# FFN down projection of a decoder layer: a wait for each inner piece, and the sum of squares inside a tile's product

## The reference

```
x = x + ffn(layernorm(x))
gate, up = split(x_ln @ ternary(w_gate_up).T)      # 2 x 2048
h   = silu(gate) * up                              # 896 rows x 2048
hn  = h * rsqrt(mean(h*h) + eps)
out = hn @ ternary(w_proj).T                       # 2048 -> 512
```

## Time and profile before

| | |
|---|---|
| median of 3 runs | 1248.84 us (1247.83 to 1251.47) |
| the profiled execution | 1249.16 us |
| its span, first to last instruction | 1247.4 us |
| mean granted clock of TensorE | 0.978 |
| FFN products, first L1150 to last L1218 | 1071 to 1245 us |

### The profile page before, as it was taken

One profiled execution on the slowest core, in us unless ns is written; L12 is line 12 of the kernel. 1 busy time (PEld: TensorE's weight loads), 2 busy tenths in 40 slices (PEclk: granted clock), 3 DMA queues, 4 the chain that ended last, 5 costly groups with the idle time before them and its releaser, 6 DMA issues.

```text
span 1247.4 us, 19243 instructions
## 1 busy us (share of the span) xinstructions
PE 1177.8 (94%) x6330; PEld 782.0 (63%) x6330; DVE 934.7 (75%) x2785; ACT 804.9 (65%) x2295; POOL 619.6 (50%) x769
## 2 busy tenths in 40 slices
PE   4999989889999999999999999999999998898998
PEld 2667766556666666666666676666667666454563
DVE  4669988999889888798999976557777877464241
ACT  4666557777778886667666775567777677662230
POOL 2537875644544555555556732126444445266171
PEclk9989989899999999999999999999999999999999
DMA  8210001212110221213233121041011110000000
GB/s 266 86 58 26 24 17 33 84 35 69 52 51 18 64 93 47 76 43 105 89 109 94 60 87 38 17 144 59 27 50 60 42 35 1 1 1 0 35 1 26
DMA packets 27475, 69.26 MB, mean 56 GB/s; under 512 B 2944, under 2 KB 9216, under 8 KB 27376
## 3 DMA queue, kind: packets, MB, share of 16 engines
q1 hardware_dynamic: 27104, 67.67, 17.2%
q10 hardware_dynamic: 272, 0.36, 0.1%
HBM read 61.21 MB, written 6.82 MB: 55 GB/s over the span
## 4 chain that ended last, share of the span: by engine, by line
PE 57%; DVE 26%; ACT 11%; POOL 3%; issue 2%; DMA 1%; ACTq 0%; POOLq 0%; SPq 0%
PE ps L870 14%; PE ps L1150 8%; PE ps L1081 7%; PE ps L860 6%; PE ps L1029 5%; PE ps L962 4%; PE ps L1202 4%; DVE big L982 3%; DVE big L415 3%; ACT big L799 3%; PE ps L994 3%; PE ps L810 2%; DVE big L662 2%; DVE big L663 2%; DVE big L342 2%
## 5 line engine op out<-in xcount | busy, mean ns | idle before, releaser
L870 PE MATMUL ps<-big 128*125 128x512 bf16 x1152 | 264.6, 379 | 0.0
L799 ACT ACTIVATE big<-ps,big 112x128 f32<-112x128 f32 (+1 forms) x512 | 192.8, 457 | 73.6 <-POOL big L433 71.0
L870 PEld LDWEIGHTS ps<-big 128*125 128x125 bf16 x1152 | 155.2, 136 | 80.1 <-ACT big L957 0.3
L432 POOL TENSOR_TENSOR big<-big 112x4 f32<-112x4 f32 (+1 forms) x128 | 38.5, 301 | 311.2 <-ACT big L427 311.2
L860 PE MATMUL ps<-big 128*112 128x512 bf16 x768 | 188.9, 390 | 4.3 <-ACT big L957 1.7
L666 POOL TENSOR_TENSOR big<-big 128x448 f32<-128x448 bf16 x96 | 102.9, 1071 | 102.8 <-DVE big L979 63.6
L860 PEld LDWEIGHTS ps<-big 128*112 128x112 bf16 x768 | 100.3, 133 | 69.8 <-issue 7.9
L982 DVE TENSOR_SCALAR big<-big 112x112 f32<-112x112 f32 (+1 forms) x256 | 133.5, 542 | 6.8
L965 ACT ACTIVATE big<-ps,big 112x375 f32<-112x375 f32 x128 | 74.8, 584 | 84.3 <-DVE big L964 83.2
L415 DVE BATCH_NORM_STATS2 big<-ps 112x6 f32<-112x128 f32 (+1 forms) x512 | 113.3, 283 | 18.3 <-PE ps L870 17.0
L1029 PE MATMUL ps<-big 125*128 125x224 f32 (+1 forms) x512 | 121.3, 359 | 3.9 <-DVE big L1011 3.1
(11 more groups left out here) (115 smaller groups left out, 2291.0 us busy)
## 6 DMA issues: line engine op xcount, KB each, us to landing
big<-in_ctx_t SPq DMA_DIRECT2D x32, 375.0 KB, 3.4
big<-in_w_s SPq DMA_DIRECT2D x16, 512.0 KB, 4.1
big<-in_w_p SPq DMA_DIRECT2D x16, 512.0 KB, 4.4
big<-in_w_x SPq DMA_DIRECT2D x16, 512.0 KB, 3.7
big<-in_w_g SPq DMA_DIRECT2D x16, 512.0 KB, 3.7
big<-in_w_d SPq DMA_DIRECT2D x8, 512.0 KB, 4.3
big<-in_w_a SPq DMA_DIRECT2D x8, 384.0 KB, 4.7
scr<-big SPq DMA_DIRECT2D x24, 128.0 KB, 1.7
```

The lines of the kernel that those rows point to most:

```text
L799: t = act(lambda e, j=j: e.activation(z[0:rows, 128 * j:128 * j + 128], bk[0:rows, 128 * j:128 * j + 128], ACT.Identity, bias=rr[0:rows, 4 ...
L870: t = pe(lambda e, k=k, s=s, u=u, n=n: e.matmul(bk[0:CK, :], cT[:, s, k, CK * c:CK * c + CK], w[:, u, k, col:col + 512], start=n == 0, sto ...
```

## The change

Two edits in `d_0`. Matmul n waits for `hd[j][n]`, the token of the piece that it reads, in place of the whole list. And the matmul that sums the squares, with the taking of its bank, moves from behind the 32 matmuls to between them: behind 28 of them in tiles 0 and 4 (the first tile of each half), behind 8 in the others. What follows it (L1210, L1213, and `d_1`) is written in the same order as before.

```diff
@@ -1201,11 +1201,12 @@
                 for h in ffn_h[j][m]:
                     t = pe(lambda e, m=m, h=h, n=n: e.matmul(
                         bk, h[:, sl], wd[:, m, :], start=n == 0, stop=n == 31),
-                        hd[j], free, ready["d"], signal=n == 31)
+                        hd[j][n], free, ready["d"], signal=n == 31)
                     n += 1
-            ri, (rk, _), rfree = bank.take()
-            tr = pe(lambda e: e.matmul(rk[:, 0:1], acc[j][:, sl], cf[:, C_UNIT:C_UNIT + 1], start=True, stop=True),
-                    accs[j], rfree)
+                    if n == (28 if b % 4 == 0 else 8):
+                        ri, (rk, _), rfree = bank.take()
+                        tr = pe(lambda e: e.matmul(rk[:, 0:1], acc[j][:, sl], cf[:, C_UNIT:C_UNIT + 1],
+                                                   start=True, stop=True), accs[j], rfree)
             si, sm, sf = small2.take()
             t1 = dve(lambda e: e.tensor_scalar(sm[:, 0:1], rk[:, 0:1], 1.0 / 2048.0, RMS_EPS, ALU.mult, ALU.add),
                      tr, sf)
```

## The result

| | before | after |
|---|---|---|
| median of the runs | 1249.12 us (4 runs) | 1238.12 us (1237.18 to 1239.65, 4 runs) |
| ratio, with its 95% interval | | 0.9914 (0.9899 to 0.9928) |
| the profiled execution, its span | 1249.16 us, 1247.4 | 1239.65 us, 1237.9 |

The forecast was 1238.8 us. In the changed kernel L1207 is now L1208, L1210 L1211, L1213 L1214 and L1218 L1219.

What follows compares the result with a forecast made beforehand. TensorE, busy 94% of the span, was taken to bound the kernel, with time lost where it idled. Terms 4.1 + 1.4 + 2.2 + 1.7 + 0.7 − 0.1 = 10.0 us gave 1238.8 us, range 1236.8 to 1243.0.

Steps and rivals of the forecast that it cites:

- The gaps, 4.1 and 2.2 us: Ahead of each half's first down projection tile, PE's stream runs on without idling: 4.1 and 2.2 us saved.
- The clock, 1.4 and 1.7: Both first tiles run at granted clock 1.00 once no gap stands ahead of them: 1.4 and 1.7 us saved.
- The end, 0.7: At the kernel's end, L1218 waits for the last product alone, the sum's steps being done earlier: 0.7 us saved.
- The waits, 0.1: About twenty added waits at the ends of both first tiles, all met: 0 to 0.4 us cost, 0.1 taken.
- The rival by which each waiting load is exposed: In the first tiles, about twenty waits expose weight loads: 2.0 us back (1240.8) or 4.8 (1243.6); chance 0.07.
- The sum of squares, 0.2: In all 7 tiles, the two-pass matmul costs PE the same 0.2 us wherever it stands.
- The thin margin at n = 28: First half's first tile: POOL's last addition ends 0.8 us before the sum of squares is due.
- Does the first half's gain last: Behind the first tile, L1109's input chain moves forward with PE, 1.9 us to spare; the gain reaches the second half.
- the clock's other cause: Rival: in the first tiles the clock stays low for another reason, 3.1 us don't come back, 1241.9; chance 0.06.
- an eaten gain: Rival: another late input between 1143 and 1176, or POOL's late sum, loses up to 5.5 us, 1244.3; chance 0.06.
- a change that doesn't do what it says: Rival: wrong pieces or another input keeps the first-tile gap; only the end's 0.7 us remain, 1248.1; chance 0.03.

Runs made afterwards that it cites:

- The first edit alone: Kernel before, with matmul n waiting for piece n only and the sum of squares left behind the 32 matmuls: 1240.68 us, ratio 0.9931.
- the run with the sum at 8: Changed kernel with the sum of squares behind 8 matmuls in every tile, also the first of each half: 1244.06 us, ratio 0.9960 to the kernel before.
- the second edit alone: Changed kernel with every matmul waiting for the whole list again, the sum of squares still moved: 1249.05 us, ratio 0.9993 to the kernel before.
- the 224 waits: Changed kernel with a wait for its own piece ahead of each of the 224 down projection matmuls: 1239.36 us, ratio 0.9913 to the kernel before.
- the filled gaps: Kernel before, with 18 and 9 unread matmuls ahead of the first tiles of the first and second half: 1245.60 us, ratio 0.9971.

## Why the prediction was right

*The gaps, 4.1 and 2.2 us*: right. 4.10 measured; the second half's gap and clock together 3.96 for 3.9. The first edit alone shows both gaps gone. The end of PE's stream moved from 1243.2 (1236.14 + 7.07) to 1234.6, 8.6 us.

*The clock, 1.4 and 1.7*: the sum was right, 3.1, and so was the mechanism; its parts were a reading of one execution. I took it that a low stretch begins exactly behind each gap. At the first gap it began inside: the stretch of the gap itself, which the earlier trace rows leave out, has 0.94.

```profile
1139.10:1143.00 3.90, 0.00 (x1) 0.00 (x0) 3.17 (x3) 1.91 (x2) 3.60 (x4) 0.94 0.00 0
```

Nor does a low stretch follow each gap. Four executions give about 2.6 on average for the first gap and 0.4 for the second, and the run with the sum at 8 had a gap of 3.3 us with none. That the four sums lie between 2.9 and 3.1 us saved the forecast; I had no reason to expect it, and none of these runs says why it should be so.

*The end, 0.7*: 0.78 in the trace; by time, the second edit alone can't be told from nothing.

*The waits, 0.1*: about 20 were added, as counted, and ten times as many cost nothing measurable. The rival by which each waiting load is exposed gave 2.0 us; the bank waits of the earlier trace rows were the better guide.

*The sum of squares, 0.2*: too much, without consequence. L1207 starts 0.14 us ahead of the next tile (1228.96 to 1229.10), and 32 matmuls take 6.90 us (1141.11 to 1148.01 in the run with the first edit alone), not 6.83.

*The thin margin at n = 28*: 0.8 us was forecast, and it is not a constant. POOL ended 0.3 us ahead of L1208 in the profiled execution and 0.9 ahead in the changed kernel's second profile and in the run with a wait at every matmul. PE waited in none. At n = 8 the gaps were 4.4 us.

*Does the first half's gain last*: yes. From L1081 on nothing was late, and L1109 follows L1100 by the same 1.9 us (1155.3 to 1157.2).

Of the rivals, the exposed loads fall with the 224 waits; the clock's other cause falls with the filled gaps; an eaten gain and a change that doesn't do what it says fall with the profile after.

## What to carry to other kernels

Where one wait holds an engine for the last of many inputs although its first instructions need only the first, give each instruction its own wait: a wait that is met cost nothing measurable here, and the stream covers the tail of the producers. An idle TensorE costs its gap and, often, a stretch at a low clock (five of the eight gaps of 2.06 and 3.92 us here), so a gap that can't be closed is worth filling, and its clock should be read from several executions, not from one. Work that only feeds a later step belongs behind the work that can cover its wait: moved too little, the wait only moves with it.

## What was not expected of the hardware

The low clock behind a gap is not a fixed price. The gap of 2.06 us had a low stretch in one execution of four, one of 3.31 us in the middle of a tile had none, and the 3.9 us gap had stretches that cost 1.4 to 3.0 us. In the filled gaps and behind them the clock was at its full level. What decides between them is open; the gaps differ in what PE did before them, and no run here varied that alone.
